# A graph layer whose gathered tiles all go through GpSimd, with no single-row fetches from SyncE and ScalarE

## The reference

```python
w_ij = silu(edge_feats @ rad_W1 + rad_b1) @ rad_W2 + rad_b2
w_ij = w_ij + (silu(chi_scalar @ sph_W1 + sph_b1) @ sph_W2 + sph_b2)
q_i = (x @ Wq)[receivers];  k_j = (x @ Wk)[senders];  v_j = (x @ Wv)[senders]
alpha = (q_i * w_ij * k_j).sum(per head of 16) / 4 * cutoffs
out = segment_sum(alpha * v_j, receivers, 6250) / 16
x = layernorm(x + out)
```

## Time and profile before

| | us |
|---|---|
| median of 3 runs | 3080.48 |
| lowest and highest | 3071.52, 3084.78 |
| the profiled execution's own time | 3072.67 |
| its span, first to last instruction | 3070.5 |

### The profile page before, as it was taken

How to read it: one execution, slowest core, us unless ns; L and a number is a source line. 1 busy time by engine, 2 the same in 40 slices (tenths; PEclk the granted TensorE clock), 3 DMA queues, 4 the chain that set the end, 5 groups by cost and what they waited for, 6 DMA issues and landing times.

```text
span 3070.5 us, 57668 instructions
## 1 busy us (share of the span) xinstructions
PE 1841.5 (60%) x14110; PEld 1454.5 (47%) x14110; DVE 1579.4 (51%) x4351; ACT 719.4 (23%) x1030; POOL 1477.7 (48%) x1561
## 2 busy tenths in 40 slices
PE   6366655665656565656556665656565555665557
PEld 5254444454544444444444554444454444454446
DVE  3155554555545554545555555555454454555547
ACT  3122222222222222222222222222222222222223
POOL 6525445544545444445544454554454444544541
PEclk8677777877787777777877777777777787777778
DMA  7434333333333333333333343333333334333331
GB/s 248 145 105 119 109 108 120 113 107 116 106 114 109 109 109 108 114 100 119 111 109 117 101 119 108 111 117 103 117 109 108 117 102 116 112 110 115 103 116 50
DMA packets 180549, 349.26 MB, mean 114 GB/s; under 512 B 68077, under 2 KB 87512, under 8 KB 180216
## 3 DMA queue, kind: packets, MB, share of 16 engines
q0 software_dynamic: 73808, 201.03, 22.7%
q1 hardware_dynamic: 96294, 137.01, 13.9%
q10 hardware_dynamic: 10114, 7.54, 0.9%
HBM read 330.47 MB, written 14.95 MB: 112 GB/s over the span
## 4 chain that ended last, share of the span: by engine, by line
another core or an unknown queue 35%; PE 26%; DVE 21%; issue 15%; ACTq 1%; DVEq 1%; ACT 0%; DMA 0%; SPq 0%
PE bank L737 16%; DVE t L1047 5%; PE bank L755 3%; DVE msg L1067 3%; DVE t L1034 2%; DVE oh L938 2%; DVE ot L932 2%; DVE accT L988 2%; DVE part L962 2%; PE bank L780 2%; ACTq L848 1%; PE bank L727 1%; PE hidden L323 1%; PE hidden L714 1%
## 5 line engine op out<-in xcount | busy, mean ns | idle before, releaser
L699 POOL DMA_INDIRECT kvt<-kvtab,srcS x1519 | 1441.0, 949 | 1519.3 <-DVE msg L1067 1074.9
L1034 DVE TENSOR_TENSOR t<-bank,kvt 128x512 f32<-128x512 f32 (+1 forms) x395 | 263.6, 667 | 1074.2 <-remote 862.1
L755 PE MATMUL bank<-msg,oh 128*32 128x128 f32 x3200 | 210.4, 341 | 962.7 <-DVE accT L988 916.1
L826 ACT ACTIVATE hs<-hidden,B 128x1024 f32<-128x1024 f32 x404 | 427.0, 1108 | 1419.0 <-remote 897.2
L737 PE MATMUL bank<-W2r,hs 128*128 128x128 f32 x3224 | 625.4, 354 | 25.2 <-ACT bank L832 15.0
L755 PEld LDWEIGHTS bank<-msg,oh 128*32 128x32 f32 x3200 | 79.3, 121 | 1160.9 <-issue 1085.5
L737 PEld LDWEIGHTS bank<-W2r,hs 128*128 128x128 f32 x3224 | 536.7, 252 | 128.1 <-issue 82.5
L737 PE MATMUL bank<-W2s,hs 128*128 128x128 f32 x3224 | 556.6, 330 | 0.0
L737 PEld LDWEIGHTS bank<-W2s,hs 128*128 128x128 f32 x3224 | 530.0, 249 | 0.0
L832 ACT ACTIVATE bank<-b2f 128x512 f32<-128x512 f32 x401 | 241.3, 602 | 840.2 <-DVE t L1034 554.4
L1049 DVE TENSOR_REDUCE coef<-t 128x32 f32<-128x512 f32 x402 | 275.8, 686 | 13.9
(11 more groups left out here) (134 smaller groups left out, 710.0 us busy)
## 6 DMA issues: line engine op xcount, KB each, us to landing
kvA<-kvtab ACTq DMA_DIRECT2D x4352, 1.0 KB
kvS<-kvtab SPq DMA_DIRECT2D x3968, 1.0 KB
dbt<-dst SPq DMA_DIRECT2D x102, 512.0 KB, 5.1
eft<-in_ef SPq DMA_DIRECT2D x102, 512.0 KB, 6.3
kvt<-kvtab,srcS POOLq DMA_INDIRECT x1519
qwt<-qtab SPq DMA_DIRECT2D x202, 32.0 KB
kvtab<-kvt SPq DMA_DIRECT2D x24, 256.0 KB, 2.0
qtab<-qx SPq DMA_DIRECT2D x12, 384.0 KB
```

Source lines behind the costliest of these rows:

```text
L699: pool.indirect_dma_start(kvt[:, (g - HX) % KS, t, :], None, kvtab, bass.IndirectOffsetOnAxis(ap=srcS[:, g * TG + t:g * TG + t + 1], axis= ...
L755: m = pe.matmul(strips(g)[32 * t:32 * t + W, 0:D], oh[:, g % WS, t, :], msg[:, g % MS, t, :], start=True, stop=True)
L826: act.activation(hs[:, 2 * p % HS:2 * p % HS + n, j, :], hidden[:, 0:2 * n, :].rearrange("p (a j) f -> p a j f", j=2)[:, :, j, :], ACT.Sil ...
L1034: m = dve.tensor_tensor(t1[:, s, a:b, :], tiles(WB[s][:, :])[:, a:b, :], kv[:, :, 0:D], ALU.mult)
```

## The change

`RS` and `RA` become 0. The row tables of SP and ACT are then empty, `at_s` and `at_a` hold no group, and all 1,584 tiles of the main loop (1,612 with the 28 of the first groups) are fetched by GpSimd. The other lines keep the code valid for a rate of zero. The SiLUs of 1,024 columns and ACT's bias copies are as they were.

```diff
-RS, RA = 40, 44
+RS, RA = 0, 0
@@ registers
-    return -(-(others + most) // 4) * 4
+    return max(4, -(-(others + most) // 4) * 4)
@@ row_tiles
+    if not rate:
+        return at
@@ act_rows
-                    if g % BA == at and a < e:
+                    if g % BA == at and a < e and at_a:
```

## The result

The changed kernel takes 2731.85 us (median, 2710.06 to 2762.11); the kernel before, on the same chip in turn with it, 3076.63 (3071.52 to 3084.78). The ratio is 0.8846, 95% interval 0.8818 to 0.8874: 345 us faster by the medians, where 45 us slower was forecast and 3030 was the lower end of the range.

A forecast was written before the change was run, and what follows sets the result against it. The prediction took the kernel to be bound by PE results held back during GpSimd's bursts of gathers. Gathers +68, DVE -10, ACT -13 and SP 0 gave +45 us on the median 3080.48, so 3125 us, range 3030 to 3168.

The forecast's parts named there:

- What bounds the kernel: Main loop: while GpSimd's gathers run close together, PE's results are held back and DVE waits, 880.3 us at L1034.
- The control: Stage without gathers, 160 to 187 us: 3.72 us a group despite single rows, against 7.38 in the long stage.
- rival A: Main loop: without single rows holds start later, four groups a cycle, not three; about 2790 at most, 2930 if half; chance 0.20.
- The gathers' term: GpSimd, main loop: 65 added gathers lengthen the holds on PE at 1.05 us each, +68 us.
- The failed step: Single-row transfers removed: 3,968 on SP put at 0, 4,352 on ACT at -13 us, gained at the start.
- Rival B: Main loop: added gathers fit in GpSimd's 1,074.9 us of waiting, so no change, 3070 us; chance 0.15.
- The gatherless stage of 3.72 us: The stage from 160 to 187 us, 3.72 us a group, cited against rival B's no change.
- the rule it rests on: Trainium skill: issuing from several engines only saves a sequencer's issue time, so moving rows gains nothing where no issuer is full.
- DVE's and ACT's terms: DVE's unsplit instructions in 65 groups, -10 us (bounds -19 and 0); ACT's removed rows at the start, -13 (-22 and 0).
- my three terms (+45): Whole kernel: added gathers +68, DVE's unsplit instructions -10, ACT's removed rows -13, sum +45 us.

The follow-up runs named there:

- e9: Kernel before with its single rows kept, but SP loads each group's rows in one transfer of neighbouring rows instead of GpSimd's main-loop gathers; 2156.26 us, ratio 0.7004.
- e15: Changed kernel with a 128x512 memset on GpSimd behind each main-loop gather; 2745.93 us, ratio 0.8832 to the kernel before.
- e3: Kernel before with all tiles gathered by GpSimd; SP and ACT still fetch their single rows, which DVE does not read; 2093.68 us, ratio 1.0326.
- r1: The changed kernel run again beside the kernel before; 2773.96 us against 3105.14, ratio 0.8902.
- e5: Kernel before with each of SP's and ACT's 65 tiles fetched by one transfer of neighbouring rows; 2670.99 us against 3105.14, ratio 0.8587.
- e10: Kernel before with all tiles gathered and all row transfers kept, each moving 64 bytes that DVE does not read; 3182.99 us, ratio 1.0322.
- e8: Changed kernel with two register moves in the place of each former row transfer; 2745.82 us, ratio 0.8945 to the kernel before.
- e11: Kernel before without ACT's single rows, SP's kept and GpSimd gathering ACT's tiles; 3042.68 us beside 3082.14, ratio 0.9877.
- e1: Kernel before without ACT's single rows, SP's kept and GpSimd gathering ACT's tiles; 2048.9 us beside 2026.96, ratio 1.0115.
- e2: Kernel before without SP's single rows, ACT's kept and GpSimd gathering SP's tiles; 2044.36 us beside 2026.96, ratio 1.0092.
- e16: Kernel before, single rows kept, with a 128x512 memset behind each of GpSimd's main-loop gathers; 2613.11 us beside 2028.88, ratio 1.2884.
- e6: Kernel before with GpSimd waiting for steps of DVE before the second to fourth gather of a group; 2770.31 us beside 3105.14, ratio 0.8912.

## Why the prediction was wrong

**What bounds the kernel: right.** While gathers run close together, results of PE are held, and a hold ends some 1.8 us behind the burst. e9 (no gathers, no holds) and e15 (gathers apart, no holds) show it.

**The control: misread.** The stage without gathers at 3.72 us a group showed that rows alone hold nothing, which e9 confirms. I concluded that "the gathers, not the single rows, double the time of a group". The control can't say that: it has rows without gathers, and the question was rows beside gathers. The set-up, gathers without rows, was the other corner, and the earlier trace rows had PE doing eight matmuls eight microseconds into the burst. I gave that only to rival A.

**The gathers' term: about right.** +68 us was forecast (62 to 81). It is 67 in condition 2 (e3), and in condition 1 some 100 (r1 against e5, e10 against the kernel before), 1.5 to 1.6 each, above my upper price of 1.25. Each of these pairs also joins DVE's split instructions, so the gathers alone may cost up to 19 us more. Why one costs more than its issue step in condition 1 is not shown.

**The failed step: the removed rows.** I costed SP's at 0 and ACT's at -13. The kernel without them, with one transfer for each tile in their place, is 434 us faster (e5); with the 103 us of the added gathers that makes up the 331 us of that series, and 345 in the result. I looked for what their issue costs in ACT's own queue, and for a wait that names SP's loads; the price stands in neither. It could be seen in the earlier trace rows, which I quoted: eleven row transfers of ACT, which have a median of 0.235 us, take 5.38 us, 0.49 each. SP's queue says it still more plainly in the trace of the kernel before, inside the hold and behind it:

```profile
1506.16 5.80 SPq L625 DMA_DIRECT2D kvS<-kvtab  x9
...
1516.93 1.28 SPq L625 DMA_DIRECT2D kvS<-kvtab  x4
```

0.64 us each while PE's results are held, 0.32 after. The rows stood in the same jam as PE, and so did the register moves between them: in the trace's single records of this hold a move at 1509.78 and a transfer at 1511.26 last 0.70 us each, and 0.70 is also the step of PE's lone matmuls in the set-up. That the rows suffer doesn't yet show that they cause; e5 and e8 show that.

**Rival A: right in sign and size, with another working.** Its bound was about 2790 with all of it, 2930 with half, and it had a chance of 0.20. The measured 2731.85 lies 58 us beyond its bound (which by its own terms comes to about 2780). Its title, that the rows bring the hold forward, is what the two timelines show. Its count is half right: I had three groups between two holds become four. Counting GpSimd's pauses of over 2 us in the long stage of the two traces, there are 233 before, 12.1 us and 1.64 groups apart on average, and 189 after, 13.2 us and 2.01 groups apart (12.1 / 1.64 = 7.38, 13.2 / 2.01 = 6.57 us a group). So more groups do pass in a cycle, by a factor of 1.22 where I had 1.33, but the cycles are of one or two groups and not of three or four. Nor is that count what costs: e11, with SP's rows, has 190 such pauses and the same 2.01 groups between them, but 14.7 us for each cycle, and takes 7.31 us a group. (The result that I called held "about three us into the burst" was given 1.95 us into it, 1504.88 to 1506.83.) "Against it" I had the harsh hold in the set-up; it is still there and costs nothing new.

**Rival B: wrong.** GpSimd's waiting fell by 387 us and not by 81, and DVE's with it. The gatherless stage of 3.72 us, which I held against the rule it rests on, says nothing of that rule, since no row changes its engine there.

**DVE's and ACT's terms.** The start lost its 7.36 us group, as said. The 19 us at most for DVE's split are too small to be told apart in these runs.

**The size depends on the condition.** Where the kernel before takes 2,027 us, the sum of my three terms (+45) is close to what e1 and e2 add up to (+39). That is luck more than insight: my 68 us were for longer holds on PE, and there nothing is held; the gathers cost what they take in GpSimd's full queue. The changed kernel itself was not run there.

**Open.** Which resource PE's results and the row transfers share; why the cost saturates at half the rows or fewer; whether it vanishes when the gathers stand apart (e16 met the other condition); how large the gap must be between 0.38 and 0.71 us; and what makes the two conditions. Every execution here was recorded for its span and clock, so a part of that recording in the holds is not excluded either.

## What to carry to other kernels

A stage with one suspect alone doesn't acquit it in company: look for the stage with each cause alone and the one with both before a cost is set to zero. Where an engine waits for something unnamed, compare the duration of every other queue's small operations inside and outside of that wait; one that stretches there is in the same jam, and taking it away may pay more than its own time. Where gathers and small transfers run beside PE, measure under the condition that the kernel will meet: here one edit is worth -11% in one and about +2%, by adding up two parts, in the other.

## What the runs showed of the hardware

- With GpSimd's indirect gathers about 1.25 us apart, in condition 1, results of PE are held until some 1.8 us behind the last gather of a burst. In the bursts of eight shown, the first held result was given 1.95 us into the burst with single rows and 6.8 us into it without (1485.87 to 1492.70); with 0.71 us free between the gathers they pass.
- In the set-up the single matmuls that pass start at multiples of 0.7 us (97.54, 100.34 and 103.14 are 4 x 0.70 apart). In a hold SP's queue is as slow, its register moves included (up to 1,387 ns in e11, 37 in e1).
- In condition 1, 8,320 transfers of one row beside gathers cost some 1.1 us a group (434 us / 403), with 64 bytes in each as with 1,024. Some 4,000 of them cost most of that: about 95% from ACT alone or from both engines, 80% from SP alone.
- The same program takes 2,027 us or 3,105 us, each series within 1%. Of the kernel of e1 and e11 there is a trace in both conditions: 2048.0 us at a mean granted clock of 0.915, 3040.8 us at 0.766. The clock alone is not what holds: in e15 nothing is held at 0.816, and in e6 results are held for 884 us in all at 0.809.
